# An order table for every engine, and score steps taken one head pair at a time, in a fused cross-attention kernel on one core

## The chip, the cores and the metric

The kernel runs on one core of a Trainium2 chip. The metric is the device time of one launch in microseconds (us). Three runs of the kernel before took 802.34 us in the median (801.8 to 805.32).

A core has five engines that run side by side, each through its own instructions in their order, and that wait for each other by semaphores: TensorE (PE, matmuls), VectorE (DVE), ScalarE (ACT), GpSimd (POOL) and SyncE (SP), which here only issues DMAs.

## The reference

Two batches of 2048 query rows of width 640 attend with 20 heads of 32 to 146 text keys, and, in a second softmax with a mask, to 8 image keys. Both results are added, projected and added to the input:

```python
q = _split_heads(hidden_states @ w_q, HEADS)
k = _split_heads(text @ w_k, HEADS)
v = _split_heads(text @ w_v, HEADS)
out_text = _merge_heads(_sdpa(q, k, v))
k_ip, v_ip = _split_heads(ip_h @ w_k_ip, HEADS), _split_heads(ip_h @ w_v_ip, HEADS)
out_ip = _merge_heads(_sdpa(q, k_ip, v_ip, mask=mask_ip))   # mask from bounding boxes
out = (out_text + IP_SCALE * out_ip) @ w_out + b_out + residual
```

## The kernel before, in words

The 4096 query rows are worked on in 16 blocks of 256 rows (two halves of 128, called qt). After a setup (keys, values, mask), iteration t of a loop works on two blocks at once: the "front" half of block t, the "back" half of block t-1, and the input transposes of block t+1 ("next"). Iteration 0 has no back half, and at its places TensorE also makes the values for the setup (`make_values`, at the steps in `V_PLACES`). Iteration 16 has only the back half. Iterations 1 to 15 have front and back, and all but the fifteenth the next stage too.

The products are in split precision: a number is held as a high part and a low part, ScalarE makes the high part and VectorE the rest by a subtraction. The 20 heads form 5 groups g of 4. The steps are:

- X u: TensorE transposes a part of the next block's input `x_in`; ScalarE and VectorE make `xt_hi`, `xt_lo`.
- Q g: 15 matmuls make the queries of a group; ScalarE writes `q_hi`, VectorE `q_lo`. DMAs (SP's STK 0 for groups 0 to 2, STK 1 for groups 3 and 4, 13 DMAs each) put them head by head into `q_stack`.
- S g, qt: scores of a group's four heads, in two pairs; each pair fills one of two PSUM banks, and VectorE takes the maxima (two reductions, `neg_max`). The next pair but one waits until they are taken. After the last of a set of groups VectorE splits the maxima (`max_parts`; SPLIT in the new tables).
- AUX n: TensorE transposes the maxima, VectorE copies them out (`aux_a`, `aux_b`), and SP copies them by DMA under the queries, so that a second product gives scores minus maxima.
- ST g, u: that product, transposed: u = 0 and 1 are two heads each, u = 2 the tail keys. ScalarE takes exp (`p_whole`, `p_hi`, or `p_tail`), and for u < 2 VectorE computes `p_lo` = `p_whole` - `p_hi`, both of which lie in SBUF. The ST steps take turns in two PSUM banks, `scores_t`.
- PV g, qt: probabilities times values. VectorE normalises (a reciprocal and two multiplications into `o_parts`), GpSimd adds the three parts into `attn` (L450, L455). PV waits for the group's `p_lo`, and for the normalising of the previous group in the same bank.
- AT qt, u: transposes of `attn` (`at_hi`, `at_lo`); O qt, half: the output projection, 15 matmuls; VectorE adds `x_res` and writes `out_sb`, SP stores it.

GpSimd also adds the bias to `x_res` (L459, 128x1280). SP loads `x_in` for the next block (L385) and `x_res` (L390), the latter after the stores of the block before have landed.

What sets the order is a table written out by hand, `STEPS` (L75). TensorE, ScalarE, VectorE and GpSimd all go through this one table, each doing its part of every step; VectorE alone takes the ST steps two places later (`late`). SP has a fixed program of its own (L372 to L418).

Of the kernel before, what the change touches and what calls it, by code (L numbers as in the profile page):

```python
# [39 lines left out]
P = 128  # L40
# [53 lines left out]
V_PLACES = {("X", 0): (0, 1), ("S", 1, 0): (2, 3), ("S", 2, 0): (4, 5), None: (6, 7)}  # L94
W_O_PLACE = ("S", 2, 0)
# [4 lines left out]
SCORES = {"S": 2}  # L100
# [11 lines left out]
class Iteration:  # L112
# [17 lines left out]
    def steps(self, late=None):  # L130


        gen = sc = 0
        steps = []
        for stage, kind, *args in STEPS:
            if stage in self.stages:
                steps.append((stage, kind, args, gen, sc))
                gen += GENERAL.get(kind, 0)
                sc += SCORES.get(kind, 0)
        if late:  # L140
            places = [i + 0.5 + late[1] if step[1] == late[0] else i for i, step in enumerate(steps)]
            steps = [steps[i] for i in sorted(range(len(steps)), key=lambda i: places[i])]
        return steps
# [20 lines left out]
def attention_kernel(nc, x, ctx, boxes, wq, wk, wv, wk_ip, wv_ip, wo, b_out,  # L164
# [5 lines left out]
    with ExitStack() as stack:  # L170
# [135 lines left out]
        def _(sp):  # L306
# [65 lines left out]
            def body(it):  # L372
                t = it.t
                for n, groups in enumerate((SET_A, SET_B)):
                    if it.back:

                        sp.wait_ge(gen_freed, it.gen_after("AUX", n))
                        for i, g in enumerate(groups):
# [3 lines left out]
                    if n == 0 and it.next:  # L382
# [4 lines left out]
                if it.back:  # L387

                    sp.wait_ge(stored, t * 16 * QT)
                    sp.dma_start(x_res[:], x_rows[bass.ds(t * QB - QB, QB), :].rearrange("(a p) d -> p a d", p=P)  # L390
                                 ).then_inc(xr_loaded, 16)
                if not it.back:

                    sp.wait_ge(s_klo, 2 * GROUPS)
                    keys_to_stack(0)
                for n, groups in enumerate((SET_A, SET_B)):
                    g0, g1 = groups[0], groups[-1] + 1
                    if it.front:
# [373 lines left out]
        def _(pe):  # L772
# [94 lines left out]
            def body(it):  # L867
# [7 lines left out]
                for stage, kind, args, gen, sc in it.steps():  # L875
# [50 lines left out]
                    if kind == "ST":  # L926
# [132 lines left out]
```

## Time and profile before

| | |
|---|---|
| profiled execution | 801.8 us, and its span as well 801.8 us |
| TensorE busy | 732.8 us (91%) |
| VectorE busy | 565.4 us (71%) |
| ScalarE busy | 287.3 us (36%) |
| GpSimd busy | 237.1 us (30%) |
| mean granted TensorE clock | 0.981 of full speed |
| chain that ended last | PE 59%, DVE 18%, SPq 9%, issue 7%, DMA 7%, ACT 1% |

The busy time of TensorE counts matmuls from start to modelled end, so gaps shorter than the drain of a matmul (some 0.2 us) don't show in it; they show as idle time ahead of the next weight load (PEld). The program falls into three parts: the setup with iteration 0 up to 117.0 us, fifteen full iterations up to 760.9 us, and the back half of the last block up to 801.8 us. An iteration can be told in the timeline by the transposes of AUX 0 (L923 on `max_parts_a`), which open it.

### The profile page before, as it was taken

Reading aid. Unit: us, or ns where it says so; the run is one execution under the profiler, and the core shown is the slowest. Engines: PE = TensorE matmul, PEld = TensorE weight load, DVE = VectorE, ACT = ScalarE, POOL = GpSimd, SP = SyncE. Lnnn points to the kernel's source line nnn. Section 1 sums busy time; section 2 is a strip of 40 time slices with the busy share of each in tenths; the row PEclk is TensorE's granted clock in tenths of the full one; section 3 lists DMA queues with packets and bytes.
Section 4 is the critical chain, followed back from the end, with each engine's and each line's share of the span. In section 5 each row is a group of like instructions: output and inputs, shape, how many; then the busy total and the mean of one; then the engine's idle time right before and its main releaser. Section 6 shows DMA issues by size and latency. Waiting matters only on the chain.

```text
span 801.8 us, 19010 instructions
## 1 busy us (share of the span) xinstructions
PE 732.8 (91%) x6384; PEld 645.1 (80%) x6384; DVE 565.4 (71%) x1694; ACT 287.3 (36%) x615; POOL 237.1 (30%) x347
## 2 busy tenths in 40 slices
PE   5968979999999999999999899999999999999887
PEld 4755458888888898989898888888898989898766
DVE  3241287778786968687878777786968686878774
ACT  1111026253443525151616152443525151616051
POOL 1000143324150606042423324150606051423334
PEclk9969999999999999999999999999999999999979
DMA  9989714344343525342424344343525342423220
GB/s 257 268 242 220 168 26 109 93 109 112 98 106 86 133 77 129 92 116 80 126 80 118 86 117 108 99 106 85 133 77 131 89 119 80 126 80 93 76 67 34
DMA packets 85115, 91.27 MB, mean 114 GB/s; under 512 B 10768, under 2 KB 69776, under 8 KB 85068
## 3 DMA queue, kind: packets, MB, share of 16 engines
q1 hardware_dynamic: 85084, 90.87, 43.6%
q8 instruction: 18, 0.29, 0.2%
q14 instruction: 13, 0.11, 0.0%
HBM read 40.42 MB, written 10.62 MB: 64 GB/s over the span
## 4 chain that ended last, share of the span: by engine, by line
PE 59%; DVE 18%; SPq 9%; issue 7%; DMA 7%; ACT 1%; DVEq 0%; ACTq 0%
PE psum L864 30%; PE psum L913 7%; PE psum L958 4%; SPq L407 4%; PE psum L939 4%; DVE p_lo L730 4%; PE psum L944 3%; DMA q_stack<-aux_a 3%; DVE o_parts L745 3%; DVE inv_den L737 2%; PE psum L835 2%; DMA q_stack<-mask_scratch 2%; DVE neg_max L706 2%; PE psum L982 2%; PE psum L799 2%
## 5 line engine op out<-in xcount | busy, mean ns | idle before, releaser
L450 POOL TENSOR_TENSOR attn<-o_parts 128x128 f32<-128x128 f32 x160 | 72.9, 456 | 443.0 <-DVE o_parts L742 443.0
L706 DVE TENSOR_REDUCE neg_max<-psum 128x2 f32<-128x292 f32 x320 | 144.1, 451 | 18.0 <-PE psum L913 14.8
L864 PE MATMUL psum<-wo_both,at_hi 128*128 128x320 f32 x640 | 154.1, 313 | 0.0
L730 DVE TENSOR_TENSOR p_lo<-p_whole,p_hi 128x512 f16<-128x512 f32 x160 | 137.1, 857 | 2.4 <-ACT p_hi L553 0.9
L913 PE MATMUL psum<-k_stack,q_stack 104*128 104x154 f32 x640 | 108.5, 284 | 20.0 <-DVE neg_max L707 13.4
L542 ACT ACTIVATE q_hi<-psum 128x256 fp32r<-128x256 f32 x80 | 30.7, 384 | 258.5 <-PE psum L864 258.5
L958 PE MATMUL psum<-v_tail,p_tail 128*128 128x264 f32 x320 | 105.5, 411 | 17.8 <-DVE p_lo L730 15.8
L864 PE MATMUL psum<-xt_hi,wq_hi 128*128 128x256 f32 x400 | 115.2, 288 | 1.0 <-DVE xt_lo L675 1.0
L913 PEld LDWEIGHTS psum<-k_stack,q_stack 104*128 104x128 f32 x640 | 89.6, 193 | 31.3 <-DVE neg_max L707 22.1
L864 PE MATMUL psum<-xt_lo,wq_hi 128*128 128x256 f32 x400 | 113.1, 283 | 0.0
L864 PE MATMUL psum<-xt_hi,wq_lo 128*128 128x256 f32 x400 | 113.0, 283 | 0.0
L552 ACT ACTIVATE p_whole<-psum 128x512 f32<-128x512 f32 x160 | 95.9, 599 | 44.2 <-PE psum L939 40.6
L864 PEld LDWEIGHTS psum<-wo_both,at_hi 128*128 128x128 f32 x640 | 109.7, 188 | 0.0
L455 POOL TENSOR_TENSOR attn<-attn,o_parts 128x128 f32<-128x128 f32 x160 | 104.8, 655 | 12.5
L864 PE MATMUL psum<-wo_both,at_lo 128*128 128x320 f32 x320 | 98.6, 308 | 0.0
L553 ACT ACTIVATE p_hi<-psum 128x512 f16<-128x512 f32 x160 | 95.6, 598 | 0.0
L697 DVE TENSOR_TENSOR q_lo<-psum,q_hi 128x256 fp32r<-128x256 f32 x80 | 34.0, 424 | 78.5 <-ACT q_hi L542 78.5
L763 DVE TENSOR_TENSOR out_sb<-psum,x_res 128x320 f32<-128x320 f32 x64 | 31.4, 491 | 66.4 <-PE psum L864 66.4
L864 PEld LDWEIGHTS psum<-xt_hi,wq_hi 128*128 128x128 f32 x400 | 77.2, 193 | 1.3 <-issue 1.3
L864 PEld LDWEIGHTS psum<-xt_hi,wq_lo 128*128 128x128 f32 x400 | 77.2, 193 | 0.0
L864 PEld LDWEIGHTS psum<-xt_lo,wq_hi 128*128 128x128 f32 x400 | 76.8, 192 | 0.0
L939 PE MATMUL psum<-q_stack,k_stack 120*128 120x256 f32 x320 | 69.8, 309 | 4.6 <-DMA q_stack<-aux_a 3.9
(87 smaller groups left out, 1331.4 us busy)
## 6 DMA issues: line engine op xcount, KB each, us to landing
q_stack<-q_hi SPq DMA_DIRECT2D x128, 96.0 KB
x_in<-in_x SPq DMA_DIRECT2D x16, 640.0 KB, 4.1
x_res<-in_x SPq DMA_DIRECT2D x16, 640.0 KB, 4.0
out<-out_sb SPq DMA_DIRECT2D x32, 320.0 KB
q_stack<-q_hi SPq DMA_DIRECT2D x128, 64.0 KB
q_stack<-q_lo SPq DMA_DIRECT2D x64, 96.0 KB
q_stack<-q_lo SPq DMA_DIRECT2D x64, 64.0 KB
q_stack<-aux_a SPq DMA_DIRECT2D x48, 64.0 KB, 2.3
```

The source lines that it names most:

```text
L407: sp.dma_start(q_stack[row:row + DH, 4 * g0 + j:4 * g1:4, :].bitcast(F32), src[DH * j:DH * (j + 1), g0:g1, :].bitcast(F32)).then_inc(stack ...
L450: nc.gpsimd.tensor_tensor(cols, o_parts[:, qt, 0:4, :], o_parts[:, qt, 4:8, :], ALU.add).then_inc(att_half, 1)
L455: nc.gpsimd.tensor_tensor(cols, cols, o_parts[:, qt, 8:12, :], ALU.add).then_inc(att_done, 1)
L552: nc.scalar.activation(p_whole[:, u, :, :].rearrange("p h q -> p (h q)"), src[:], ACT.Exp)
L553: nc.scalar.activation(p_hi[:, -g % P_SLOTS, 2 * u:2 * u + 2, :].rearrange("p h q -> p (h q)"), src[:], ACT.Exp).then_inc(exp_done, 1)
L697: nc.vector.tensor_tensor(q_lo[:, g, :], bank_a[:, 0:QB], q_hi[:, g, :].bitcast(F32), ALU.subtract).then_inc(gen_freed, 1)
L706: nc.vector.tensor_reduce(dst[:, :, 0], src[:, :, 0:TEXT], AX_X, ALU.max, negate=True)
L730: nc.vector.tensor_tensor(p_lo[:, -g % P_SLOTS, 2 * u:2 * u + 2, :], p_whole[:, u, :, :], p_hi[:, -g % P_SLOTS, 2 * u:2 * u + 2, :], ALU.s ...
L864: last = nc.tensor.matmul(ps, l(c), r(c), start=(i == 0), stop=(i == len(terms) - 1))
L913: last = nc.tensor.matmul(scores[(sc + pair) % 2][:, i * CTX:(i + 1) * CTX], q_stack[0:ROW_MAX, h, P * qt:P * (qt + 1)], k_stack[batch][0: ...
L939: last = nc.tensor.matmul(ps[:, QB * i:QB * (i + 1)], k_stack[batch][0:STACK, h, 0:P], q_stack[0:STACK, h, :], start=True, stop=True)
L958: nc.tensor.matmul(product_1[qt][:, 0:8, :], p_tail[:, -g % P_SLOTS, queries], v_tail[batch][:, g, :].rearrange("p (e d) -> p e d", d=VW), ...
```

## The change

1. `STEPS` is a new order, and a score step is one pair of heads, S g, qt, pair, so that another step can stand between the two pairs.
2. ScalarE, VectorE, GpSimd and SP get tables of their own: `ACT_STEPS`, `DVE_STEPS`, `POOL_STEPS`, `SP_STEPS`. ScalarE keeps to `STEPS` in iteration 0. The split of the maxima is a step of VectorE's own table.
3. The ST steps take their banks in the order of the table (`ST_TURN`), no longer by 3g + u; the tail step of a group often comes before or between its other two.
4. The bias addition on GpSimd (XR) moves from the end of an iteration to its start, and the load of `x_res` on SP from behind the `aux_b` DMAs to ahead of them.

```diff
@@ STEPS, a line or two of it; the tables of the other engines are new
-    (NEXT, "X", 0), (BACK, "PV", 4, 0), (BACK, "PV", 4, 1), (FRONT, "S", 0, 0), (BACK, "AT", 0, 0), (BACK, "AT", 0, 1),
+    (BACK, "PV", 4, 1), (BACK, "AT", 0, 0), (FRONT, "S", 0, 1, 0), (BACK, "AT", 0, 1), (FRONT, "S", 0, 1, 1),
+    (NEXT, "X", 0), (NEXT, "X", 1), (FRONT, "S", 1, 0, 0), (BACK, "AT", 1, 0), (FRONT, "S", 1, 0, 1),
...
+POOL_STEPS = [
+    (BACK, "XR"), (BACK, "PV", 0, 0), (BACK, "PV", 0, 1), (BACK, "PV", 1, 0), (BACK, "PV", 1, 1), (BACK, "PV", 2, 0),
...
+SP_STEPS = [
+    (BACK, "AUX", 0), (NEXT, "XIN"), (BACK, "XRES"), (BACK, "AUX", 1), (FRONT, "STK", 0), (FRONT, "STK", 1),
+    (BACK, "STORE", 0), (BACK, "STORE", 1),
+]
-V_PLACES = {("X", 0): (0, 1), ("S", 1, 0): (2, 3), ("S", 2, 0): (4, 5), None: (6, 7)}
+V_PLACES = {("X", 0): (0, 1), ("S", 1, 0, 0): (2, 3), ("S", 2, 0, 0): (4, 5), None: (6, 7)}
-SCORES = {"S": 2}
+SCORES = {"S": 1}
+ST_TURN = {s[2:]: n for n, s in enumerate(s for s in STEPS if s[1] == "ST")}
+ST_ALL = len(ST_TURN)
@@ SP, the wait ahead of the query DMAs
-                            sp.wait_ge(st_ready, 15 * t - 15 + 3 * g1)
+                            sp.wait_ge(st_ready, t * ST_ALL - ST_ALL + 1 + max(ST_TURN[(g, u)] for g in groups for u in range(3)))
@@ GpSimd
-                for stage, kind, args, gen, sc in it.steps():
+                for stage, kind, args, gen, sc in it.steps(POOL_STEPS):
+                    if kind == "XR":
+                        pool.wait_ge(xr_loaded, t * 16)
+                        nc.gpsimd.tensor_tensor(x_res[:], x_res[:], bias[:].unsqueeze(1).to_broadcast([P, QT, D]),
+                                                ALU.add).then_inc(xr_ready, 1)
...
-                        if (g, qt) == (GROUPS - 1, QT - 1):
-                            pool.wait_ge(xr_loaded, t * 16)
-                            nc.gpsimd.tensor_tensor(x_res[:], x_res[:], bias[:].unsqueeze(1).to_broadcast([P, QT, D]),
-                                                    ALU.add).then_inc(xr_ready, 1)
@@ ScalarE, VectorE
-                for stage, kind, args, gen, sc in it.steps():
+                for stage, kind, args, gen, sc in it.steps(ACT_STEPS if it.back else STEPS):
-                for stage, kind, args, gen, sc in it.steps(late=("ST", 2)):
+                for stage, kind, args, gen, sc in it.steps(DVE_STEPS):
@@ TensorE, score pairs and ST banks
-                        for pair in range(2):
-                            if it.back or sc + pair >= 2:
-                                pe.wait_ge(s_freed, it.sc0 + sc + pair - 1)
+                        if it.back or sc >= 2:
+                            pe.wait_ge(s_freed, it.sc0 + sc - 1)
...
-                        if g or u > 1:
-                            pe.wait_ge(exp_done, t * 15 - 15 + 3 * g + u - 1)
-                        ps = scores_t[(3 * g + u) % 2]
+                        n = ST_TURN[(g, u)]
+                        if n >= 2:
+                            pe.wait_ge(exp_done, t * ST_ALL - ST_ALL + n - 1)
+                        ps = scores_t[n % 2]
```

First place: TensorE in iteration 0, behind its five Q steps (`wo_raw,rest_t`, `w_kv,rest_t` and `w_kv,ctx_t` are the values for the setup, `x_in` the X steps, `k_stack,q_stack` the score pairs, two matmuls each). Before:

```order
L835 MATMUL psum<-wo_raw,rest_t 16x512 x8
L835 MATMUL psum<-wo_raw,rest_t 16x128 x8
L845 MATMUL psum<-ident,x_in 128x128 x4
L913 MATMUL psum<-k_stack,q_stack 128x154 x4
L845 MATMUL psum<-ident,x_in 128x128 x6
L913 MATMUL psum<-k_stack,q_stack 128x154 x4
L835 MATMUL psum<-w_kv,rest_t 36x512 x8
```

and in the changed kernel:

```order
L951 MATMUL psum<-k_stack,q_stack 128x154 x8
L874 MATMUL psum<-wo_raw,rest_t 16x512 x8
L874 MATMUL psum<-wo_raw,rest_t 16x128 x8
L884 MATMUL psum<-ident,x_in 128x128 x8
L874 MATMUL psum<-w_kv,rest_t 36x512 x8
```

The first two value products stood ahead of the first score pairs and now stand behind four of them.

Second place: GpSimd in the loop (`attn<-o_parts` and `attn<-attn,o_parts` are the two additions of a PV step). Before, at the loop's end:

```order
L450 TENSOR_TENSOR attn<-o_parts 128x128
L455 TENSOR_TENSOR attn<-attn,o_parts 128x128
L458 REGISTER_ALU
L459 TENSOR_TENSOR x_res<-x_res,bias 128x1280
L155 REGISTER_ALU
```

In the changed kernel, at the loop's start:

```order
L191 ISA
L486 TENSOR_TENSOR x_res<-x_res,bias 128x1280
L491 ISA
L493 TENSOR_TENSOR attn<-o_parts 128x128
L498 TENSOR_TENSOR attn<-attn,o_parts 128x128
```

The bias addition stood behind the ten PV steps and now stands ahead of them.

Third place: VectorE in the loop of the changed kernel, from the last score maxima of the back half to the first two PV steps (`p_lo` is an ST step, `inv_den` opens a PV step):

```order
L755 CAST max_parts_b<-neg_max 128x32
L757 TENSOR_TENSOR max_parts_b<-neg_max,max_parts_b 128x32
L768 REGISTER_ALU
L769 TENSOR_TENSOR p_lo<-p_whole,p_hi 128x512
L768 REGISTER_ALU
L769 TENSOR_TENSOR p_lo<-p_whole,p_hi 128x512
L735 REGISTER_ALU
L736 TENSOR_TENSOR q_lo<-psum,q_hi 128x256
L763 CAST aux_b<-psum 32x256
L768 REGISTER_ALU
L769 TENSOR_TENSOR p_lo<-p_whole,p_hi 128x512
L775 ISA
```

The three `p_lo` shown are those of ST 0,1, ST 1,0 and ST 1,1. Before, a third `q_lo` (that of Q 3) stood between the last of them and PV 0,0, and from PV 0,0 on one PV step and one `p_lo` took turns; now two PV steps of group 0 come one behind the other.

## Rows read from the trace of the kernel before

**Rows 1.** Windows: times busy per engine, granted clock, DMA share, GB/s; three stretches.
```profile
332.35:375.03 42.68, 40.60 (x381) 36.88 (x379) 33.35 (x102) 17.10 (x37) 13.95 (x21) 1.00 0.39 104
204.10:760.90 556.80, 525.68 (x4918) 478.40 (x4917) 432.36 (x1323) 220.20 (x478) 181.20 (x273) 1.00 0.39 103
760.90:801.80 40.90, 32.39 (x272) 27.86 (x269) 25.23 (x69) 13.99 (x29) 14.27 (x21) 0.87 0.17 49
```
**Rows 2.** Waits of weight loads, 332.3 to 375: line, releaser, us, times, longest.
```profile
PEld psum L958 <- issue: 1.7, 3, 0.9
PEld psum L913 <- DVE neg_max L707: 1.1, 3, 0.8
PEld psum L939 <- DMA q_stack<-aux_a: 0.4, 1, 0.4
PEld psum L939 <- ACT p_tail L556: 0.3, 1, 0.3
PEld psum L982 <- POOL attn L455: 0.3, 1, 0.3
```
**Rows 3.** Timeline of TensorE in that iteration: start, length, idle before.
```profile
358.38 0.71 PE L958 MATMUL psum<-v_tail,p_tail 128*128 128x264 f32 x2 [0.69 <-DVE p_lo L730]
...
372.06 0.90 PE L913 MATMUL psum<-k_stack,q_stack 104*128 104x154 f32 x4 [0.63 <-DVE neg_max L707]
```
**Rows 4.** Timeline of TensorE in iteration 0.
```profile
67.05 8.79 PE L835 MATMUL psum<-wo_raw,rest_t 128*16 128x512 f32 x32
...
80.25 0.65 PE L913 MATMUL psum<-k_stack,q_stack 104*128 104x154 f32 x4 [3.82 <-DMA q_stack<-mask_scratch]
...
82.59 9.73 PE L835 MATMUL psum<-w_kv,rest_t 128*36 128x512 f32 x32
...
117.01 0.42 PE L923 MATMUL psum<-ident,max_parts_a 128*80 128x128 f32 x2 [2.23 <-DVE v_main L656]
```
**Rows 5.** Windows, stretch in which the granted clock was half.
```profile
81.00:84.50 3.50, 3.50 (x13) 2.01 (x11) 2.62 (x10) 0.87 (x2) 0.00 (x0) 0.51 0.40 98
```
**Rows 6.** Timeline of ScalarE, exp of the first ST step.
```profile
338.24 0.60 ACT L552 ACTIVATE p_whole<-psum 128x512 f32<-128x512 f32 x1 [0.77 <-PE psum L939]
338.73 0.59 ACT L553 ACTIVATE p_hi<-psum 128x512 f16<-128x512 f32 x1
339.21 0.61 ACT L552 ACTIVATE p_whole<-psum 128x512 f32<-128x512 f32 x1
```
**Rows 7.** Single lines of the kernel: ns min/median/max, first and last start.
```profile
L730 DVE TENSOR_TENSOR p_lo<-p_whole,p_hi x160: 679/966/977, 126.7 to 784.2; 128x512 f16<-128x512 f32 x160
```
**Rows 8.** The same for GpSimd's second addition and its bias addition.
```profile
L455 POOL TENSOR_TENSOR attn<-attn,o_parts x160: 452/782/795, 132.8 to 788.6; 128x128 f32<-128x128 f32 x160
...
L459 POOL TENSOR_TENSOR x_res<-x_res,bias x16: 2912/2940/2947, 148.5 to 789.0; 128x1280 f32<-128x1280 f32 x16
```
**Rows 9.** Timelines of VectorE and GpSimd at 106 us.
```profile
106.71 6.35 DVE L716 CAST max_parts_a<-neg_max 128x48 fp32r<-128x48 f32 x1
...
106.08 6.93 POOL L438 TENSOR_TENSOR wo_both<-wo_raw,wo_both 128x3200 fp32r<-128x3200 f32 x1 [3.65 <-ACT wo_both L528]
```
**Rows 10.** Timeline of SP's DMA queue in the same iteration.
```profile
336.22 0.41 SPq L385 DMA_DIRECT2D x_in<-in_x  x1
342.96 1.24 SPq L380 DMA_DIRECT2D q_stack<-aux_b  x2
344.50 0.41 SPq L390 DMA_DIRECT2D x_res<-in_x  x1
```
**Rows 11.** DMA issues: engine, count, KB each, us to landing.
```profile
x_in<-in_x SPq DMA_DIRECT2D x16, 640.0 KB, 4.1
```
**Rows 12.** Windows, one stretch with `x_in` on its way; last number GB/s.
```profile
338.00:339.00 1.00, 1.00 (x7) 0.65 (x6) 0.90 (x5) 0.76 (x2) 0.00 (x0) 1.00 0.88 333
```
**Rows 13.** Timeline of VectorE, one PV step from reciprocal to the next step.
```profile
346.86 0.19 DVE L737 RECIPROCAL inv_den<-psum 128x8 f32<-128x8 f32 x1
...
347.62 0.97 DVE L730 TENSOR_TENSOR p_lo<-p_whole,p_hi 128x512 f16<-128x512 f32 x1
```

More of the change, by code:

```diff
@@ L128, in __init__, with steps, last_scores @@
         self.parity = (self.gen0 if isinstance(t, int) else GEN_N - GEN_B) % 2
-    def steps(self, late=None):
+    def steps(self, table=STEPS):
         gen = sc = 0
-        steps = []
+        at = {}
         for stage, kind, *args in STEPS:
             if stage in self.stages:
-                steps.append((stage, kind, args, gen, sc))
+                at[(kind, *args)] = (gen, sc)
                 gen += GENERAL.get(kind, 0)
                 sc += SCORES.get(kind, 0)
[L140 to L143, printed above, removed]
+        return [(stage, kind, args, *at.get((kind, *args), (0, 0)))
+                for stage, kind, *args in table if stage in self.stages]
+    def last_scores(self, n):
+        return max(sc for _, kind, args, _, sc in self.steps() if kind == "S" and args[0] == (SET_A, SET_B)[n][-1])
     def gen_after(self, kind, *args, use=0):
@@ L373, in body @@
                 t = it.t
-                for n, groups in enumerate((SET_A, SET_B)):
-                    if it.back:
+                if not it.back:
+                    sp.wait_ge(s_klo, 2 * GROUPS)
+                    keys_to_stack(0)
+                for stage, kind, args, gen, sc in it.steps(SP_STEPS):
+                    if kind == "AUX":
+                        n = args[0]
                         sp.wait_ge(gen_freed, it.gen_after("AUX", n))
-                        for i, g in enumerate(groups):
+                        for i, g in enumerate((SET_A, SET_B)[n]):
                             src = aux_rows[n][16 * i:16 * (i + 1), :].bitcast(F32).unsqueeze(1).to_broadcast([16, 4, QB])
@@ L381, in body @@
                                          ).then_inc(aux_in[n], 16)
-                    if n == 0 and it.next:
+                    if kind == "XIN":
                         sp.wait_ge(xt_ready, t * NX + NX)
@@ L386, in body @@
                                      ).then_inc(x_loaded, 16)
[L387 to L398, printed above, removed]
+                    if kind == "XRES":
+                        sp.wait_ge(stored, t * 16 * QT)
+                        sp.dma_start(x_res[:], x_rows[bass.ds(t * QB - QB, QB), :].rearrange("(a p) d -> p a d", p=P)
+                                     ).then_inc(xr_loaded, 16)
+                    if kind == "STK":
+                        n = args[0]
+                        groups = (SET_A, SET_B)[n]
+                        g0, g1 = groups[0], groups[-1] + 1
                         sp.wait_ge(gen_freed, it.gen_after("Q", g1 - 1))
                         if it.back:
-                            sp.wait_ge(st_ready, 15 * t - 15 + 3 * g1)
+                            sp.wait_ge(st_ready, t * ST_ALL - ST_ALL + 1 + max(ST_TURN[(g, u)] for g in groups for u in range(3)))
                         for row, part in STACK_PARTS:
@@ L900, in body @@
                     if kind == "S":
-                        g, qt = args
-                        if qt == 0 and g in (SET_A[0], SET_B[0]):
+                        g, qt, pair = args
+                        if (qt, pair) == (0, 0) and g in (SET_A[0], SET_B[0]):
                             n = 0 if g in SET_A else 1
```

114 lines of the change are left out of this document (70 added, 44 removed).

## The prediction

> **What bounds the kernel now.** I read the windows first, to cut the span into parts, then the waits of one iteration, then the timelines around each wait. Times inside an iteration are given from its start, the transposes of AUX 0 at 332.35 us, and written +5.9 and so on.
>
> A full iteration lasts 42.68 us at full granted clock, and the thirteen from 204.1 to 760.9 us take 42.8 each; the last back half takes 40.9 [rows 1]. In the iteration VectorE is busy 33.35 us, ScalarE 17.1, GpSimd 13.95 [rows 1]: none of them alone sets 42.68. TensorE's matmuls cover 40.6, but that hides short gaps. The weight loads show them: TensorE stood for PV steps 1.7 us, for score maxima 1.1, for the `aux_a` DMAs 0.4, for an exp 0.3, for GpSimd's `attn` 0.3 [rows 2], together 3.8 us. The longest single ones are 0.69 us at 358.38, where PV 4,0 waits for `p_lo`, and 0.63 us at 372.06, where four score matmuls in a row wait for their banks [rows 3]. So TensorE is the bound, with 42.7 - 3.8 = 38.9 us of work that no order of steps takes away. All waits gone would give 15 x 3.8 = 57 us, 7% of the span; that is the ceiling of this change in the loop.
>
> **Iteration 0.** The tables are also read there. Before, the first two value products ran from 67.05 to 75.8 us, while the DMAs filled `q_stack`; the first score pairs came at 80.25 after only 3.82 us of idling [rows 4]. Now four pairs stand ahead of these products. The DMAs depend on none of that, so the pairs still start at 80.25, TensorE idles from 67.05 on, 13.2 us instead of 3.8, and 13.2 - 3.8 = 9.4 us of work is put behind 80.25. Behind it everything to 117.01 is a row of value products with pairs between, each product about 8.8 us of TensorE's time, and it moves as a whole; GpSimd's and VectorE's part of the setup depend on the same products and move with it. Cost: +9.4. The clock could add to it: after the 3.8 us of idling the granted clock was 0.51, its 1.2 GHz level, from 81.0 to 84.5 us [rows 5], and the product that ran into this took 9.73 us where another of the same width took 8.79 [rows 4]. The longer idling can't cost less than that 0.9, which is in the sum already, and at most a whole product at half speed, 8.8. I take nothing more, since the row next to it shows 0.9, and keep the rest for the range.
>
> **The loop without any collision.** The start of an iteration is the same on both sides up to ST 0,0, whose wait of 0.4 us for `aux_a` stays: AUX 0, its copy on VectorE and the three DMAs lead every table. Then the new order brings one wait of its own. ST 0,1 now shares a bank with ST 0,0 and needs its exp, which ends at 338.73 + 0.59 = 339.3 [rows 6], +7.0; TensorE has only two score pairs and ST 0,2 to do in between and comes at about +6.6. That is 0.4 us. PV steps now come in twos while VectorE normalises one in 347.62 - 346.86 = 0.76 us [rows 13], about what TensorE needs for one: 0.1 at PV 1,1. Single front pairs leave VectorE time to free the banks between AT, X and O steps, so the 1.1 us of score waits shrink; I keep 0.3 for AT 1,0 and S 1,0,1, which come while VectorE works off PV 4,1, a pair and `at_lo`. PV 4,0 now has Q 4 ahead of it, and its `p_lo` is long done. Waits: 0.4 + 0.4 + 0.1 + 0.3 = 1.2, so 38.9 + 1.2 = 40.1 us an iteration, 2.6 less than before. VectorE would be at 33.35 / 40.1 = 83%, which it can carry. The SP queue has room: STK 0 needs all ST steps of groups 0 to 2, and in the new table none of group 3 or 4 and one Q step fewer stand ahead of the last of them, so `q_stack` is refilled before S 0,0,0.
>
> **The bias addition on GpSimd.** This is what speaks against the change. Before, `x_res` was loaded from 344.50, +12.2, and GpSimd added the bias behind its last PV step; nothing waited for it. Now SP issues this load directly behind that of `x_in` (336.22 [rows 10]), about 0.7 us later, at +4.6. `x_in` takes 4.1 us to land [rows 11], until +8.0, and the engines then move 333 GB/s [rows 12], so another 640 KB need 640 / 333 = 2.0 us: `x_res` is there at +9.9. GpSimd has nothing before it, starts, and is busy for 2.94 us [rows 8], until +12.9.
>
> In this stretch VectorE comes to its `p_lo`, with both inputs in SBUF. The rows show what such an instruction does beside a GpSimd addition: `p_lo` takes 0.68 us at least, but 0.97 in the median [rows 7], where one of GpSimd's 0.45 us additions had started just before it; and that addition's successor stretches from 0.45 to 0.78 [rows 8], as the `p_lo` then runs first. At 106.71 a CAST of only 48 columns took 6.35 us, exactly until GpSimd's addition of 6.93 us was over [rows 9]. So one waits for the other's whole instruction. The Trainium skill says the same in SBUF — State Buffer, section "Who interferes with whom": a VectorE instruction with two SBUF inputs contends with a GpSimd instruction that reads SBUF, through a shared read interface, and whoever is second "fully blocks". By that rule the whole 2.94 us is closed to `p_lo`; by a mere sharing of bandwidth it would be closed to none, and the sum would be the one without collision. The trace agrees with the rule, by the 6.35 us.
>
> Which `p_lo` is hit? An exp pair of an ST step takes 339.21 - 338.24 = 0.97 us [rows 6]. ST 0,1 starts at +7.1, its exp begins at +7.6, that of ST 1,0 at +8.5 and ends at +9.6, and its `p_lo` starts at +9.7, just ahead of `x_res`. So GpSimd waits for it and runs from +10.3 to +13.3. The `p_lo` of ST 1,1 is due at +11.1 and now ends at +13.9. Behind it on VectorE queue PV 0,0 and PV 0,1, 0.76 us each [rows 13], until +15.4; PV 1,1 on TensorE waits for the second one, and would have started at +13.9. It starts at +15.5: 1.6 us lost, and as TensorE has nearly no idle time later in the iteration, they aren't made up. If `x_res` lands some 0.3 us earlier, the `p_lo` of ST 1,0 is caught as well, and the loss is 2.0. The bounds are 0 (it falls beside instructions that read PSUM) and 2.9 (all of it on the path); between them the nearest rows give 1.6 to 2.0. Per iteration: 2.6 - 1.8 = 0.8 us gained, over 15 iterations 12.
>
> **The last back half.** No Q, X or front steps: VectorE is the bound for much of it, the order spares TensorE little, and `x_res` comes earlier still (no `x_in` ahead) and blocks the first `p_lo` there. Against that, XR is out of the way at the end. I take +0.5, between -1 and +2.
>
> **Sum.** 801.8 + 9.4 - 12 + 0.5 = 799.7 us. The profiled execution is 0.5 us under the median of 802.34, so this is 800.2 against it; I say 800. What a measurement of this kernel can tell from no change is about 0.5%, 4 us: faster is below 798.3, slower above 806.4.
>
> **The rivals.**
>
> A, no loss by the bias addition: `x_res` lands at a time when VectorE does only work that reads PSUM, or the lost time is made up in later waits. For it: only two or three of VectorE's instructions in that stretch have both inputs in SBUF. Against it: the 2.94 us are longer than any gap between them. Time: 801.8 + 9.4 + 0.5 - 15 x 2.6 = 773.
>
> B, slower: the bias addition starts before the `p_lo` of ST 1,0. Then behind this `p_lo` also stand `q_lo` of Q 2 and the copy of `aux_b`, whose DMAs (1.24 us of issue, rows 10) start about 3 us late, and ST 3,0 waits for them as well as the PV steps. The price is 2.6 to 2.9 us an iteration, the whole gain or more: 801.8 + 9.4 + 0.5 + 15 x (0 to 0.3) = 812 to 816. It decides from 2.2 us of loss on (15 x (2.6 - 2.2) = 6 against 10), where the time passes 806. For it: it takes an `x_res` only 0.3 to 0.5 us earlier than I work out.
>
> C, the value products are hidden after all, because something else sets the end of iteration 0 (the key copies or GpSimd's weight part): 800 - 9.4 = 791. Against it: 9 of the 13 us of idling are new in an order that is fixed, and before TensorE idled only 2.23 us at the end of this part [rows 4].
>
> That the change does not do what it says is no case: the order shows the split pairs and the moved bias addition.
>
> **Chances.** The forecast 0.52, with a range of its own from 790 to 809 (0.4 us an iteration either way, and the clock); 0.20 of that is below 798.3, 0.24 inside, 0.08 above 806.4. A 0.18, B 0.18, C 0.07, something else 0.05 (0.02 the same, 0.03 slower). Faster 0.20 + 0.18 + 0.07 = 0.45, same 0.24 + 0.02 = 0.26, slower 0.08 + 0.18 + 0.03 = 0.29. The range goes from 774 to 813: it leaves out the lower half of A and the upper third of B.
>
> **What would show it.** First scores of iteration 0 at about 80 us and the first AUX 0 at 126 instead of 117: the setup term. Iterations of 41.9 us (40.1 if A, 42.7 or more if B). One `p_lo` an iteration of about 2.9 us, beside the 2.94 us of GpSimd's addition, which starts at +10: the collision. A wait of TensorE of 1.5 us or more at PV 1,1 or just before, for VectorE. And 0.4 us at ST 0,1 for ScalarE. I am wrong if no `p_lo` is longer than 1 us, if the first AUX 0 stays at 117, or if new waits show in the front score pairs, where I expect next to none.

## The result, and the profile after

The changed kernel takes 807.99 us in the median of 13 runs (804.03 to 811.48); the kernel before, run beside it, 802.86 us (800.67 to 805.32). The ratio is 1.0058, with a 95% interval of 1.0041 to 1.0074: slower by 0.6%. The forecast was 800. The profiled execution took 807.99 us with a span of 806.2 us; the span of the kernel before was 801.8. All times and ratios here and below are those of fast executions; three of the 24 executions of the two filler kernels further down, more than 1.5% above the fastest of their kernel, are left out.

The page of the changed kernel: busy time by engine, and the granted clock in 40 slices of 20 us:

```profile
PE 728.2 (90%) x6384; PEld 651.8 (81%) x6384; DVE 584.7 (73%) x1694; ACT 289.7 (36%) x615; POOL 238.2 (30%) x347
...
PEclk9967799999999999999999999999999999999979
```

VectorE is busy 19 us more than before (565.4) on the same work.

Windows of the changed kernel, columns as in [rows 1]: the fifteen full iterations, the last back half, one iteration of the quick kind, one of the slow kind, and two stretches at half clock:

```profile
131.18:764.89 633.71, 599.02 (x5676) 558.75 (x5677) 516.99 (x1527) 256.91 (x552) 210.69 (x315) 0.98 0.38 104
764.89:806.20 41.31, 31.49 (x272) 27.13 (x269) 26.48 (x69) 14.03 (x29) 13.82 (x21) 0.87 0.17 49
342.40:383.69 41.29, 39.29 (x382) 36.75 (x380) 34.10 (x102) 17.13 (x37) 14.72 (x21) 1.00 0.39 107
213.65:257.05 43.40, 40.84 (x381) 37.82 (x379) 35.16 (x102) 17.21 (x37) 13.46 (x21) 0.96 0.37 102
71.80:88.90 17.10, 7.30 (x15) 2.76 (x16) 1.99 (x8) 0.00 (x0) 0.00 (x0) 0.50 0.66 116
228.74:232.14 3.40, 3.40 (x29) 2.61 (x30) 2.92 (x8) 0.29 (x1) 2.85 (x6) 0.51 0.61 130
```

The three parts against [rows 1, 4]: setup and iteration 0 end at 131.18 instead of 117.01 (+14.2); the fifteen iterations take 633.7 instead of 643.9 (-10.2); the last back half takes 41.3 instead of 40.9 (+0.4). Sum +4.4, which is the difference of the spans.

The cut at AUX 0 moves one thing from one part to the other. In the kernel before, the first full iteration took 44.40 us and not 42.7, because a stretch at half clock, from 118.5 to 122.0 us, fell into it:

```profile
117.01:161.41 44.40, 42.10 (x379) 38.47 (x380) 33.05 (x102) 17.18 (x37) 13.96 (x21) 0.96 0.37 96
```

In the changed kernel such a stretch came at 119.6 to 123.0 us, still ahead of AUX 0, and its first iteration kept the full clock. So 1.7 us of the +14.2 were paid before as well, only behind the cut.

Timeline of TensorE in iteration 0, which answers to [rows 4]:

```profile
81.39 1.11 PE L951 MATMUL psum<-k_stack,q_stack 104*128 104x154 f32 x4 [13.95 <-DMA q_stack<-mask_scratch]
...
83.80 11.30 PE L874 MATMUL psum<-wo_raw,rest_t 128*16 128x512 f32 x32
...
96.06 8.80 PE L874 MATMUL psum<-w_kv,rest_t 128*36 128x512 f32 x32
...
119.06 10.55 PE L874 MATMUL psum<-w_kv,ctx_t 128*128 128x512 f32 x32
131.18 0.41 PE L961 MATMUL psum<-ident,max_parts_a 128*80 128x128 f32 x2 [1.57 <-issue]
```

TensorE idles 13.95 us ahead of the first scores, as forecast. But the scores come 1.1 us later than before, and two products ran partly at the 1.2 GHz level: 11.30 us where 8.79 is the full-clock time, and 10.55 where the same product took 8.85 in the kernel before.

The loop. Timelines of VectorE and of GpSimd in the quick iteration, which began at 342.40:

```profile
352.07 0.69 DVE L769 TENSOR_TENSOR p_lo<-p_whole,p_hi 128x512 f16<-128x512 f32 x1 [0.29 <-ACT p_hi L592]
352.68 0.41 DVE L736 TENSOR_TENSOR q_lo<-psum,q_hi 128x256 fp32r<-128x256 f32 x1
353.01 0.40 DVE L763 CAST aux_b<-psum 32x256 fp32r<-32x256 f32 x1
353.48 2.61 DVE L769 TENSOR_TENSOR p_lo<-p_whole,p_hi 128x512 f16<-128x512 f32 x1
```

```profile
352.27 3.27 POOL L486 TENSOR_TENSOR x_res<-x_res,bias 128x1280 f32<-128x1280 f32 x1 [21.36 <-DMA x_res<-in_x]
```

The bias addition starts at +9.87 (forecast +9.9), is behind the `p_lo` of ST 1,0 by 0.2 us, and holds that of ST 1,1, which starts at +11.1: it takes 2.61 us and ends 0.55 us after the addition, where alone it takes 0.69. The addition itself takes 3.27 instead of 2.92 us behind the first `p_lo`. `q_lo` and the CAST, which read PSUM, pass untouched. In the slow iteration, which began at 213.65, GpSimd came first, by 0.13 us (VectorE, then GpSimd):

```profile
223.31 3.34 DVE L769 TENSOR_TENSOR p_lo<-p_whole,p_hi 128x512 f16<-128x512 f32 x1 [0.29 <-ACT p_hi L592]
```

```profile
223.18 2.92 POOL L486 TENSOR_TENSOR x_res<-x_res,bias 128x1280 f32<-128x1280 f32 x1 [21.02 <-DMA x_res<-in_x]
```

Waits of weight loads, the first rows of the quick iteration and of the slow one, as in [rows 2]:

```profile
PEld psum L997 <- DVE o_parts L784: 1.5, 1, 1.5
PEld psum L978 <- ACT p_hi L592: 0.4, 1, 0.4
PEld psum L978 <- DMA q_stack<-aux_a: 0.4, 1, 0.4
PEld psum L1021 <- DVE at_lo L792: 0.3, 1, 0.3
```

```profile
PEld psum L997 <- DVE o_parts L784: 2.1, 1, 2.1
```

This is the wait at PV 1,1, forecast at 1.6. In the slow iteration the clock falls right behind it (0.51 from 228.74 to 232.14, in the windows above), and the PV step there takes twice its time:

```profile
226.34 0.48 PE L978 MATMUL psum<-q_stack,k_stack 120*128 120x256 f32 x2
228.74 1.18 PE L997 MATMUL psum<-v_tail,p_tail 128*128 128x264 f32 x2 [1.92 <-DVE o_parts L784]
```

Of the fifteen iterations the bias addition caught the `p_lo` of ST 1,0 in eight, that of ST 1,1 in six. In the six of the second kind TensorE's wait (of the weight load, as above) is 1.3 to 1.6 us, and they last 41.2 to 41.6. In the eight it is 2.0 to 2.2 (in one of them the profile shows it on the matmul alone, 1.8); two of them last 41.8 and 41.9 at a clock of 1.00, and six, each with such a stretch at half clock, 43.4 to 43.55.

In the fifteenth no `x_in` is loaded, the addition starts at +7.6, and what it catches is no `p_lo` but the cast of the maxima, which takes 0.18 us elsewhere (VectorE, then GpSimd):

```profile
731.90 2.58 DVE L755 CAST max_parts_b<-neg_max 128x32 fp32r<-128x32 f32 x1
```

```profile
731.52 2.92 POOL L486 TENSOR_TENSOR x_res<-x_res,bias 128x1280 f32<-128x1280 f32 x1 [19.08 <-DMA x_res<-in_x]
```

TensorE waits 1.28 us for it at AUX 1. The same happens in the last back half (cast 2.31 us, wait 0.82).

### The profile page after: what moved, and what is told of

Its sections match the earlier page's. It is cut to its first block, busy times and chain, and to the rows that moved or that the text cites. A ratio compares the mean times of both kernels' runs of the same rounds, so it can differ in the third digit from the quotient of the medians.

```text
span 806.2 us, 18997 instructions
## 1 busy us (share of the span) xinstructions
PE 728.2 (90%) x6384; PEld 651.8 (81%) x6384; DVE 584.7 (73%) x1694; ACT 289.7 (36%) x615; POOL 238.2 (30%) x347
## 4 chain that ended last, share of the span: by engine, by line
PE 59%; DVE 12%; issue 10%; SPq 7%; DMA 7%; ACT 4%; DVEq 0%; ACTq 0%
PE psum L903 27%; PE psum L997 7%; PE psum L978 5%; PE psum L874 5%; DMA q_stack<-aux_a 4%; PE psum L951 4%; ACT p_hi L592 3%; PE psum L983 2%; SPq L421 2%; PE psum L1005 2%; SPq L445 2%; PE psum L838 2%; DVE p_lo L769 2%; PE psum L1006 2%; PE psum L1021 2%
## 5 line engine op out<-in xcount | busy, mean ns | idle before, releaser
L769 DVE TENSOR_TENSOR p_lo<-p_whole,p_hi 128x512 f16<-128x512 f32 x160 | 154.2, 966 | 19.3 <-ACT p_hi L592 17.5
L486 POOL TENSOR_TENSOR x_res<-x_res,bias 128x1280 f32<-128x1280 f32 x16 | 47.7, 2982 | 329.6 <-DMA x_res<-in_x 329.6
L951 PE MATMUL psum<-k_stack,q_stack 104*128 104x154 f32 x640 | 112.4, 284 | 19.3 <-DMA q_stack<-mask_scratch 14.5
L493 POOL TENSOR_TENSOR attn<-o_parts 128x128 f32<-128x128 f32 x160 | 90.6, 566 | 100.6 <-DVE o_parts L781 98.9
L951 PEld LDWEIGHTS psum<-k_stack,q_stack 104*128 104x128 f32 x640 | 91.4, 193 | 23.2 <-issue 14.3
L498 POOL TENSOR_TENSOR attn<-attn,o_parts 128x128 f32<-128x128 f32 x160 | 88.1, 550 | 12.5
L978 PE MATMUL psum<-q_stack,k_stack 120*128 120x256 f32 x320 | 71.9, 324 | 8.8 <-DMA q_stack<-aux_a 4.6
L1005 PEld LDWEIGHTS psum<-v_main,p_hi 128*128 128x128 f16 x640 | 58.5, 99 | 21.5 <-issue 2.5
```

What stands on the lines that cost most here:

```text
L486: nc.gpsimd.tensor_tensor(x_res[:], x_res[:], bias[:].unsqueeze(1).to_broadcast([P, QT, D]), ALU.add).then_inc(xr_ready, 1)
L493: nc.gpsimd.tensor_tensor(cols, o_parts[:, qt, 0:4, :], o_parts[:, qt, 4:8, :], ALU.add).then_inc(att_half, 1)
L498: nc.gpsimd.tensor_tensor(cols, cols, o_parts[:, qt, 8:12, :], ALU.add).then_inc(att_done, 1)
L769: nc.vector.tensor_tensor(p_lo[:, -g % P_SLOTS, 2 * u:2 * u + 2, :], p_whole[:, u, :, :], p_hi[:, -g % P_SLOTS, 2 * u:2 * u + 2, :], ALU.s ...
L951: last = nc.tensor.matmul(scores[sc % 2][:, i * CTX:(i + 1) * CTX], q_stack[0:ROW_MAX, h, P * qt:P * (qt + 1)], k_stack[batch][0:ROW_MAX, ...
L978: last = nc.tensor.matmul(ps[:, QB * i:QB * (i + 1)], k_stack[batch][0:STACK, h, 0:P], q_stack[0:STACK, h, :], start=True, stop=True)
```

## The experiments

Ratios are to the kernel before. Times are medians of five or six timed runs, of eleven and ten for the two filler kernels; positions come from one profiled execution each.

### The two parts undone, apart and together

`e1_values_first`: the first two value products stand ahead of the first scores again.

```diff
-V_PLACES = {("X", 0): (0, 1), ("S", 1, 0, 0): (2, 3), ("S", 2, 0, 0): (4, 5), None: (6, 7)}
+V_PLACES = {("S", 0, 0, 0): (0, 1), ("S", 1, 0, 0): (2, 3), ("S", 2, 0, 0): (4, 5), None: (6, 7)}
```

> The changed kernel with one edit: in iteration 0 the first two value products stand ahead of the first score pair again. Theory: in the changed kernel TensorE idles about 13.5 us for the query DMAs, and behind that 9.4 us of moved work and a stretch at half clock follow; both go. The first AUX 0 comes at 117 to 118 us instead of 131.2, the iterations behind it are as they are in the changed kernel (42.2 us in the mean), time 794 us. Rival: only the moved work comes back and the rest of the 14.2 us has another cause (DMA queue, GpSimd's part of the setup): AUX 0 at 121 to 122, time 799 us.

Measured: 795.3 us, 0.9894 (0.9867 to 0.9922), 12.7 us under the changed kernel. The time is near the 794 expected, the place is not: AUX 0 comes at 123.36, 7.8 us earlier and not 13 to 14, because three value products still met half clock (10.32, 10.55 and 10.55 us, shown below). Another 6.65 us come from the fifteen iterations (627.06 instead of 633.71), on which the edit has no hold: `p_lo` is caught in all of the first fourteen again, but only two of the iterations had a stretch at half clock, where the changed kernel's profile shows six.

`e2_bias_last`: the bias addition is behind GpSimd's PV steps again; the load stays early.

```diff
 POOL_STEPS = [
-    (BACK, "XR"), (BACK, "PV", 0, 0), (BACK, "PV", 0, 1), (BACK, "PV", 1, 0), ...
+    (BACK, "PV", 0, 0), (BACK, "PV", 0, 1), (BACK, "PV", 1, 0), ...
+    (BACK, "XR"),
 ]
```

> The changed kernel with one edit: GpSimd's bias addition stands behind the ten PV steps again; the early load of x_res stays. Theory: the addition no longer shuts p_lo out; no p_lo over 1.0 us, all full iterations at 40.1 us (they are 41.3 or 43.4 in the changed kernel), no stretch at half clock in the loop, setup unchanged at 131 us, time about 776 us. Rival 1: the new order itself makes the iterations long (VectorE late for the front score pairs), and the p_lo of 3.3 us only fill slack: iterations stay at 41.5 to 42, time 800 us or more. Rival 2: the addition at the end now delays O 0,0 through x_res, since the end of the iteration is denser: iterations of 41, time 790.

Measured: 773.12 us, 0.9613 (0.9585 to 0.964), 34.9 us under the changed kernel. The window of its fifteen iterations and of one of them, and the `p_lo` rows (ns min/median/max):

```profile
132.71:730.36 597.65, 585.85 (x5676) 550.17 (x5677) 486.01 (x1527) 256.00 (x552) 207.22 (x315) 1.00 0.41 110
332.16:371.86 39.70, 39.03 (x381) 36.68 (x379) 32.50 (x102) 17.16 (x37) 13.82 (x21) 1.00 0.41 111
```

```profile
L770 DVE TENSOR_TENSOR p_lo<-p_whole,p_hi x160: 680/718/979, 139.4 to 754.6; 128x512 f16<-128x512 f32 x160
```

No `p_lo` is longer than 1 us, VectorE's busy time in the loop falls from 517 to 486, the clock is 1.00, and an iteration takes 597.65 / 15 = 39.8 us instead of 42.2. AUX 0 comes at 132.71, 1.5 us later than in the changed kernel, as the first scores do. `x_res` is still loaded early, so it is the place of the addition that costs, and not the load. This one line is worth more than all that the change lost.

`e3_both`, both edits in one kernel:

> The changed kernel with both edits: value products ahead of the first score pair, bias addition last. Theory: the two effects lie in separate parts of the program and add up: 776 - 14 = 762 us, 5% under the kernel before. Rival: one hides part of the other (for instance, GpSimd or the DMA queue sets the end of the setup once TensorE is earlier): 767 or more.

Measured: 764.34 us, 0.9517 (0.9491 to 0.9542); the same kernel once more, `e3b_both_again`, in which only the repetition was of interest:

> The version with the value products first and the bias addition last once more (764.3 us before), so that the next two can be held against it on the same chip: 762 to 766 us, iterations of 39.8, first AUX 0 between 119 and 123.5 depending on whether a value product meets half clock (8.85 or 10.55 us).

762.98 us, 0.9506 (0.9486 to 0.9525). The two gains nearly add up: 12.7 + 34.9 = 47.6 against 43.7 and 45.0 measured. They can't quite: the 12.7 hold the 6.65 us of fewer half-clock stretches in the loop, and `e2_bias_last` has none of these left to save.

These runs also price the clock. Up to AUX 0 iteration 0 is the same code in `e1_values_first` and `e3b_both_again`. TensorE in the first, its last three products and AUX 0, then the same rows in the second:

```profile
85.01 10.32 PE L874 MATMUL psum<-w_kv,rest_t 128*36 128x512 f32 x32
...
97.68 10.55 PE L874 MATMUL psum<-w_kv,ctx_t 128*128 128x512 f32 x32
...
111.24 10.55 PE L874 MATMUL psum<-w_kv,ctx_t 128*128 128x512 f32 x32
123.36 0.41 PE L961 MATMUL psum<-ident,max_parts_a 128*80 128x128 f32 x2 [1.57 <-issue]
```

```profile
85.48 9.73 PE L875 MATMUL psum<-w_kv,rest_t 128*36 128x512 f32 x32
...
97.56 8.85 PE L875 MATMUL psum<-w_kv,ctx_t 128*128 128x512 f32 x32
...
109.42 8.85 PE L875 MATMUL psum<-w_kv,ctx_t 128*128 128x512 f32 x32
120.50 0.41 PE L962 MATMUL psum<-ident,max_parts_a 128*80 128x128 f32 x2 [2.22 <-DVE v_main L696]
```

The granted clock over the three products is 0.85, 0.84 and 0.84 in the first, and 0.90, 1.00 and 1.00 in the second. 2 x 1.70 + 0.59 us of products, less what the start and the end give back (0.47 + 0.65), is 2.9 us between two executions of one order. `e3_both`, on the same chip as `e1_values_first`, has AUX 0 at 120.18, so it isn't the chip. Part of it is again only moved: in both runs of `e3_both` a stretch at half clock falls into the first full iteration, which takes 42.2 us instead of 39.8.

### The value move alone, in the old order

`e4_before_late_values`: the kernel before, with the first two products behind the first score step.

```diff
-V_PLACES = {("X", 0): (0, 1), ("S", 1, 0): (2, 3), ("S", 2, 0): (4, 5), None: (6, 7)}
+V_PLACES = {("X", 1): (0, 1), ("S", 1, 0): (2, 3), ("S", 2, 0): (4, 5), None: (6, 7)}
```

> The kernel before with one edit: in iteration 0 the first two value products stand behind the first score pairs (at the second X step), as in the changed kernel. It tells the order's share of the setup from the rest of the new tables. Theory: idling for the query DMAs grows from 3.8 to 13 us, and the granted clock falls for longer, so 8.8 us of moved work and 2 to 4 us of half clock are added: first AUX 0 at 128 to 130 instead of 117, time 814 to 816 us. Rival, that the setup's loss in the changed kernel lies elsewhere in its tables: AUX 0 at 126 or less, time 812 or less.

Measured: 810.62 us, 1.0085 (1.0054 to 1.0115). TensorE in its iteration 0:

```profile
79.12 1.11 PE L913 MATMUL psum<-k_stack,q_stack 104*128 104x154 f32 x4 [11.83 <-DMA q_stack<-mask_scratch]
80.16 11.12 PE L835 MATMUL psum<-wo_raw,rest_t 128*16 128x512 f32 x32
...
126.95 0.41 PE L923 MATMUL psum<-ident,max_parts_a 128*80 128x128 f32 x2 [1.56 <-issue]
```

The move alone puts AUX 0 9.9 us later, although the scores came 1.1 us earlier; an iteration stays at 42.7 us. Its product, too, is at half clock for a while (11.12). This lies between the two expectations, and the time is the rival's (812 or less): 9.9 of the 14.2 us are the order of the value products, and the rest came with the other new tables.

### The bias move alone, in the old order

`e6_before_bias_first`: the kernel before, with the load of `x_res` behind that of `x_in`, and the addition ahead of GpSimd's PV steps.

```diff
+                    if n == 0 and it.back:
+                        sp.wait_ge(stored, t * 16 * QT)
+                        sp.dma_start(x_res[:], ...)
...
+                if it.back:
+                    pool.wait_ge(xr_loaded, t * 16)
+                    nc.gpsimd.tensor_tensor(x_res[:], x_res[:], bias[:] ...)
```

> The kernel before with the bias addition first on GpSimd and x_res loaded right behind x_in, its order of steps otherwise kept. Theory: the addition runs from +9.9 to +12.9 and shuts out the p_lo that come at +9.6 and +10.7; one p_lo an iteration takes 2.5 to 3.5 us, and as VectorE and TensorE go in lockstep through the PV steps behind it, 1.5 to 2.5 us an iteration are lost: 825 to 840 us. Rival: the old order has more slack there (a third q_lo and the Q 3 step stand before PV 0,0), so the p_lo is as long but costs nearly nothing: 803 to 808 us.

Measured: 824.46 us, 1.0267 (1.0232 to 1.0303). A window of one iteration, and VectorE's `p_lo` of ST 1,1 in it:

```profile
337.04:380.80 43.76, 40.66 (x381) 36.93 (x379) 35.43 (x102) 17.10 (x37) 14.46 (x21) 1.00 0.37 101
```

```profile
347.84 2.87 DVE L728 TENSOR_TENSOR p_lo<-p_whole,p_hi 128x512 f16<-128x512 f32 x1 [0.15 <-ACT p_hi L551]
```

Twelve iterations last 43.6 to 44.2 us instead of 42.7, with one long `p_lo`. The first, the eighth and the fifteenth take 45.3 to 45.8: the first has the stretch at half clock that it has in the kernel before (44.40), in the eighth the `p_lo` of ST 1,0 was caught, and in the fifteenth the last part of the maxima (`max_parts_b`, 2.94 us instead of 0.19), for which TensorE waits 1.32 us. Of the 20 us in all, 2.5 lie in the last back half. The collision costs in either order. An iteration with one long `p_lo` is 1.0 us longer in the old order and 1.5 to 1.9 in the new one; that TensorE's other waits absorb the difference is an argument, no run shows it.

### The clock in the setup

`e5_warm` and `e5b_warm_longer`: the changed kernel with 105 and 128 more matmuls of 256 columns ahead of the first scores, whose results nobody reads.

```diff
                         if (kind, *args) == ("S", 0, 0, 0):
+                            for i in range(105):
+                                nc.tensor.matmul(bank[7][:, 0:QB], wq_hi[:, i % KC, 0:P], xt_hi[:, i % KC, :],
+                                                 start=True, stop=True)
```

> The changed kernel with 105 more matmuls of 256 columns (their result is never used) on TensorE in iteration 0, in the stretch in which it waits for the query DMAs. They do no useful work and leave the order as it is. Theory that part of the setup's 14.2 us is the clock: with TensorE busy the granted clock stays at its upper level, the first value product takes 8.8 us instead of 11.3, and the first AUX 0 comes at 127.5 to 129 us instead of 131.2; time 804 to 805.5 us. Rival, that the product is slow or late for another reason (memory, DMA traffic) or that the loss is only order: AUX 0 at 131, time 808 us.

> The changed kernel with 128 instead of 105 idle-time matmuls in iteration 0 (results unused), so that TensorE has work up to the first score pair; with 105 of them 3.8 us of idling were left and the clock still fell at 81.9 us. Theory of the clock: it stays at 2.4 GHz through the first value product, which takes 8.8 us, against 11.3 in the changed kernel and 10.5 with 105; first AUX 0 at 128 to 130 us, time 804 to 806. Rival: the product stays at 10.5 or more and the time at 807.

Measured: 806.47 us, 1.0029 (1.0003 to 1.0055), and 805.42 us, 1.0027 (0.9999 to 1.0055). TensorE in the second:

```profile
83.41 0.65 PE L953 MATMUL psum<-k_stack,q_stack 104*128 104x154 f32 x4 [0.81 <-DMA q_stack<-mask_scratch]
84.47 0.95 PE L953 MATMUL psum<-k_stack,q_stack 104*128 104x154 f32 x4 [0.41 <-DVE neg_max L745]
85.34 10.39 PE L874 MATMUL psum<-wo_raw,rest_t 128*16 128x512 f32 x32
```

The scores start at full clock (0.65 us for four matmuls, 1.11 without the filler), but the clock falls in the product behind them, which still takes 10.39. From the first scores to AUX 0 it is 48.9 and 48.4 us, against 49.8 in the changed kernel and 49.6 in `e2_bias_last`, so the filler gives back about 1 us there. But the first scores came at 82.90 and 83.41 instead of 81.39, and AUX 0 at 131.8 both times, where 127.5 to 130 was expected. So the filler doesn't remove the price, and the two runs don't isolate it; intervals of these and of the changed kernel overlap.

### What else moved in iteration 0, and whether single pairs pay

`e7_x_in_early`: `e3_both` with the first `x_in` load ahead of the twelve key DMAs, where it stood before the change.

```diff
+                if not it.back:
+                    load_next()
...
-                    if kind == "XIN":
+                    if kind == "XIN" and it.back:
```

> That version with one more edit: in iteration 0 the load of x_in for the next block is issued ahead of the twelve key DMAs, as in the kernel before, and not between them and the query DMAs. Theory: those 640 KB right ahead of the query DMAs are what makes the first score pair come at 81 to 83 us instead of 79 to 80.3; it comes back to about 80, 1 to 2 us gained: 763 us. Rival: the queue is not what sets it, since the query DMAs were issued 2 us earlier in exchange; no difference, 764 us.

Measured: 761.9 us, 0.9494 (0.9471 to 0.9517), the fastest of all, though its interval overlaps that of `e3b_both_again`. TensorE:

```profile
79.48 1.11 PE L954 MATMUL psum<-k_stack,q_stack 104*128 104x154 f32 x4 [3.83 <-DMA q_stack<-mask_scratch]
...
118.50 0.41 PE L964 MATMUL psum<-ident,max_parts_a 128*80 128x128 f32 x2 [2.23 <-DVE v_main L698]
```

The first scores come 1.9 us earlier than the 81.37 of `e3b_both_again`, and AUX 0 2.0 us earlier. The time alone doesn't decide it, but the places of all profiles do: the first scores come at 79.1 to 80.3 us in the four kernels that load `x_in` ahead of the key DMAs and wait for the query DMAs, and at 80.9 to 83.4 in the eight that load it between the two.

`e8_pairs_glued`: `e3_both` with the two pairs of every score step next to each other again, in the tables of TensorE and VectorE.

```diff
+def glued(table):
+    ...
+            if s[4] == 0:
+                out += [s, (*s[:4], 1)]
+STEPS, DVE_STEPS = glued(STEPS), glued(DVE_STEPS)
```

> The version with the value products first and the bias addition last (764.3 us), with the two pairs of every score step next to each other again on TensorE and VectorE; all else of the new tables stays. It tells what the single pairs are worth. Theory: most of the 3.0 us an iteration comes from where VectorE's work stands (PV steps in twos, p_lo long before it is needed) and little from the split pairs: iterations of 40.3 to 40.8 instead of 39.8, time 771 to 780 us. Rival: the single pairs are what takes the score waits away: iterations of 41.5 to 42.5, time 790 to 805 us.

Measured: 765.61 us, 0.953 (0.9497 to 0.9563), 1.3 and 2.6 us over the two runs of `e3_both`. Iterations take 40.0 instead of 39.8 (expected 40.3 to 40.8), the fifteen together 602.35 us instead of 600.59 and 600.12. Single pairs account for about 2 us of the loop; the rest of its gain is in the order and the tables of the other engines, which no run takes apart.

`e10_values_0_to_3_first`: `e7_x_in_early` with value products 0 to 3 ahead of the first scores.

```diff
-V_PLACES = {("S", 0, 0, 0): (0, 1), ("S", 1, 0, 0): (2, 3), ("S", 2, 0, 0): (4, 5), None: (6, 7)}
+V_PLACES = {("S", 0, 0, 0): (0, 1, 2, 3), ("S", 2, 0, 0): (4, 5), None: (6, 7)}
```

> The last one with value products 2 and 3 ahead of the first score pair as well. Theory: TensorE's remaining 5 us of idling ahead of the first scores are filled; the scores come at 84.5 instead of 80 to 81, but 8.8 us of work less stand behind them, and the clock has less reason to fall there: first AUX 0 at 114 to 117 instead of 120 to 123, time 757 to 760 us. Rival: GpSimd's part of the setup (memsets after the key DMAs, then 6.9 us for the low part of the output weights) or the DMA queue becomes the end of the setup: AUX 0 stays at 119 or later, 763 us.

Measured: 765.17 us, 0.9531 (0.9513 to 0.955), slower than `e7_x_in_early`; AUX 0 comes at 124.68, where 114 to 117 was expected. Its VectorE, GpSimd and TensorE:

```profile
98.96 3.31 DVE L698 CAST v_main<-v_left 128x512 bf16<-128x512 f32 x1
...
103.43 6.43 DVE L698 CAST v_main<-v_left 128x128 bf16<-128x128 f32 x1
```

```profile
97.59 4.40 POOL L476 MEMSET k_tail<- 128x2560 uint32 x2 [94.66 <-DMA k_stack<-k_tail]
102.49 7.28 POOL L479 TENSOR_TENSOR wo_both<-wo_raw,wo_both 128x3200 fp32r<-128x3200 f32 x1 [0.50 <-ACT wo_both L569]
```

```profile
110.69 0.71 PE L954 MATMUL psum<-k_stack,q_stack 104*128 104x154 f32 x2 [10.95 <-DVE neg_max L748]
```

GpSimd's MEMSET and its long addition now lie beside two casts, which end 0.3 and 0.1 us after them and take 3.3 and 6.4 us; in `e7_x_in_early` the same casts take 0.43 and 0.23. The score maxima queue behind the casts, and TensorE waits 10.95 us: the same kind of hold as in the loop, in a new place.

## Why the prediction was wrong

It gave 800 us, with most of the chance on faster or no change; the kernel is slower by 0.6%. The step that failed is what it took for the clock: 0.9 us in iteration 0, "I take nothing more", and no term at all in the loop. Measured were 3.3 us more on the value products of iteration 0 and about 10 us in six iterations of the loop. By its own steps:

- **Iteration 0, +9.4: here the failure is open to view.** It came to +14.2. The moved product (8.8) and its idle time are as forecast. What was left out: the clock, +2.5 and +1.7 on two products less 0.9 on a third, 3.3 together; the first scores 1.1 us later; and about 1.0 us around the score pairs and X steps (1.6 in all, of which 0.6, an X step that fell behind the wait, was in the 9.4 already), less 0.7 us of wait at the end. Of the +1.7, as said above, the kernel before paid as much in its first full iteration. "I take nothing more, since the row next to it shows 0.9" took one dip as a measure for an idle time 3.7 times as long, and its bounds (0.9 to 8.8) were far apart. Rows of two executions of one code differ by 2.9 us through the clock. The later scores were missed by reading SP's new table for the loop only: in iteration 0 it puts 640 KB of `x_in` between the key DMAs and the query DMAs, and undoing that gives 1.9 us back. Of the 1.0, some 0.6 lie between the second and the third product, where single pairs now wait for maxima (0.41 and 0.60 us at 105.87 and 106.92).
- **The loop, -12:** -10.2. It is right by partly compensating errors. Without a collision the gain is 42.93 - 39.84 = 3.1 us an iteration (forecast 2.6). With the collision and at full clock, an iteration takes 41.2 to 41.9 (forecast 41.9), against 39.7; the wait of 0.4 us at ST 0,1 is there as forecast. What was not foreseen is that the collision's wait is followed by a half-clock stretch in six iterations, 1.6 us each, together 10 us. Without them, by this sum, the kernel would be at 808 - 10 = 798 us, below 802.9. This is an estimate, but `e1_values_first` bears it out: four stretches fewer, and 6.65 us less in the loop. That the sum of the loop comes out near the forecast is luck: the gain without a collision was 7 us larger than forecast, and the clock took 10.
- **The collision itself** is right in place, start, length and victim, down to the second case: the forecast said that `x_res` some 0.3 us earlier would catch the `p_lo` of ST 1,0 as well, and this happened in eight iterations of fifteen. The Trainium skill (SBUF — State Buffer, section "Who interferes with whom") calls the shared pair an exclusive lock; the 2.61 and 3.34 us of `p_lo`, and the 0.41 and 0.40 us of the two instructions that read PSUM in the same stretch, agree. The prediction's example, the CAST of 6.35 us in [rows 9], has a single input in SBUF; the case of two inputs was first seen in these `p_lo`. Taking the overlap away gives 36.1 us in the loop; less the 10 of the clock that is 26, or 1.7 an iteration, where the forecast has 1.8. Rival A's 773 us is what `e2_bias_last` took, by two errors that cancel: its first part is 6 us longer than A's, its loop 7 us shorter.
- **Rival B** was nearly right on the mechanism (ST 1,0 caught) and wrong on its price: it put 2.6 to 2.9 us on an iteration; the catch alone costs 2.1 to 2.2, little more than the other (41.8 and 41.9 us against 41.2 to 41.6), and the clock behind it brings this to some 3.7.
- **The last back half, +0.5:** +0.4, but not as argued: the bias addition there starts at +7.2 and catches the cast of the maxima and no `p_lo`.
- **From span to time:** the prediction took 0.5 us between its sum and the time. In every run on record the time is 1.7 to 1.9 us above the span of the same execution, so its 799.7 stood for about 801.5. This decides nothing.

Not settled: why two of the eight iterations in which ST 1,0 was caught kept the full clock. It doesn't hang on which `p_lo` is caught: in `e1_values_first` three of five such iterations kept it, and in `e5_warm` two iterations in which that of ST 1,1 was caught lost it, behind waits of 1.8 us on the matmul, where those of the eight are 1.8 to 2.0.

## What to carry to other kernels

Moving a long GpSimd instruction off the end of a loop is no free move: look at what VectorE reads from SBUF in the stretch where it will lie. Behind a short instruction that it delays, one line in GpSimd's table was worth 4% here. When TensorE's work is moved out of an idle stretch in front of it, count the idle time as well as the half-clock time that may follow it, and read each new table of an engine for the first iteration too. Where a profile cuts a kernel into parts, look on which side of the cut a stretch at half clock falls before the parts are compared.

## What the runs showed of the hardware

In the changed kernel a wait of TensorE's weight load of 2.0 to 2.2 us in the middle of a dense loop was followed by 3.4 us at the 1.2 GHz level in six iterations, which cost 1.6 us each; behind two more waits of this kind the clock stayed up, and in the six iterations whose wait was 1.3 to 1.6 us none followed. The same code of iteration 0 differed by 2.9 us between two executions, through the clock. A cast with a single input in SBUF was held like a `p_lo` with two (6.43 us for 128 columns beside GpSimd's addition of 7.28, 0.23 alone), and a MEMSET on GpSimd, which reads nothing, held one as well (3.31 us beside 4.40, 0.43 alone).
